# Part of a state-space scan's states summed in columns by VectorE and accumulating DMAs instead of transposed by TensorE

## What is computed

```python
u = silu(conv(in_proj_w @ ctx) + conv_b)          # [e, l]
Bm, Cm = rows of x_proj_w @ u                     # 16 x l each
delta = softplus(dt_proj_w @ dt_lo + dt_proj_b)   # [e, l]
for l:                                            # for each state n
    state[e, n] = state[e, n] * exp(delta[e, l] * A[e, n]) + delta[e, l] * u[e, l] * Bm[n, l]
    y[e, l] = sum_n state[e, n] * Cm[n, l]
y = (y + D[e] * u) * silu(layernorm(x).T)         # then transposed to [l, e]
x = x + tanh(g_xattn) * y.T
x = x + tanh(g_ffn) * (shared(ln(x)) + sum over routed e of weight_e * expert_e(ln(x)))
expert(x) = (silu(x @ W1) * (x @ Wg)) @ W2
```

## Time and profile before

| | us |
|---|---|
| median of 3 runs | 1496.21 (1495.25 to 1496.78) |
| the profiled execution | 1496.58 |
| its span, first to last instruction | 1494.5 |
| TensorE busy | 1397.6 (94%) |
| VectorE busy | 1053.1 (70%) |
| ScalarE busy | 510.0 (34%) |
| GpSimd busy | 453.6 (30%) |
| mean granted TensorE clock | 0.968 of full |

### The profile page before, as it was taken

One profiled execution on the slowest core, in us unless ns is written; L12 is line 12 of the kernel. 1 busy time (PEld: TensorE's weight loads), 2 busy tenths in 40 slices (PEclk: granted clock), 3 DMA queues, 4 the chain that ended last, 5 costly groups with the idle time before them and its releaser, 6 DMA issues.

```text
span 1494.5 us, 18163 instructions
## 1 busy us (share of the span) xinstructions
PE 1397.6 (94%) x6311; PEld 1078.6 (72%) x6311; DVE 1053.1 (70%) x1259; ACT 510.0 (34%) x855; POOL 453.6 (30%) x240
## 2 busy tenths in 40 slices
PE   8599869999999989999999979999999999999999
PEld 4244456877777776787787867787778878888887
DVE  5898855899998974588999874689999853222222
ACT  3676625544444323432322223432332211111111
POOL 3200004687777721123323211122332211111111
PEclk9599989999999999999999999999999999999999
DMA  6111634567765574455555564455555554655552
GB/s 206 43 64 57 252 121 171 204 248 272 243 244 206 212 249 141 143 192 179 177 173 181 174 247 128 143 184 179 185 176 172 184 191 156 210 194 191 189 168 84
DMA packets 90796, 266.36 MB, mean 178 GB/s; under 512 B 11472, under 2 KB 11600, under 8 KB 90336
## 3 DMA queue, kind: packets, MB, share of 16 engines
q1 hardware_dynamic: 85472, 258.39, 51.0%
q10 hardware_dynamic: 5248, 6.96, 1.3%
HBM read 207.39 MB, written 57.93 MB: 178 GB/s over the span
## 4 chain that ended last, share of the span: by engine, by line
PE 68%; DVE 18%; issue 6%; ACT 5%; DMA 2%; SPq 1%; POOL 0%; ACTq 0%; DVEq 0%; POOLq 0%
PE ps_hg L461 19%; PE ps_h L461 18%; PE ps_y L461 12%; PE ps_y L612 7%; DVE st L1098 7%; PE ps_mid L538 5%; DVE y_rows L1104 3%; ACT dA L791 2%; PE ps_h L530 2%; DVE st L1089 1%; DVE u L1000 1%; PE ps_mid L508 1%; DVE h_tmp L1224 1%; PE ps_mid L501 1%; DVE h_tmp L1219 1%
## 5 line engine op out<-in xcount | busy, mean ns | idle before, releaser
L1363 POOL TENSOR_TENSOR h_lo<-h_tmp,h_hi 128x512 fp32r<-128x512 f32 x128 | 280.8, 2194 | 781.7 <-ACT h_hi L863 781.7
L461 PE MATMUL ps_h<-x_hi,w_split 128*128 128x512 f32 x1024 | 350.8, 404 | 9.0 <-issue 4.6
L461 PE MATMUL ps_hg<-x_hi,wg_split 128*128 128x512 f32 x1024 | 349.8, 403 | 3.4 <-DVE h_tmp L1224 3.4
L1098 DVE TENSOR_TENSOR_SCAN st<-dA,st 128x1024 f32<-128x1024 f32 x128 | 298.5, 2341 | 0.0
L461 PE MATMUL ps_y<-w_split,h_hi 128*128 128x512 f32 x1024 | 258.2, 400 | 0.8 <-ACT h_hi L863 0.8
L461 PEld LDWEIGHTS ps_h<-x_hi,w_split 128*128 128x128 f32 x1024 | 195.1, 191 | 50.8 <-issue 6.9
L863 ACT ACTIVATE h_hi<-h_tmp 128x512 fp32r<-128x512 f32 x128 | 81.0, 632 | 430.6 <-DVE h_tmp L1224 430.6
L461 PEld LDWEIGHTS ps_hg<-x_hi,wg_split 128*128 128x128 f32 x1024 | 195.3, 191 | 44.4 <-issue 4.2
L461 PEld LDWEIGHTS ps_y<-w_split,h_hi 128*128 128x128 f32 x1024 | 190.3, 190 | 40.0 <-ACT h_hi L863 2.0
L1219 DVE SCALAR_TENSOR_TENSOR h_tmp<-h_tmp,ps_h 128x512 f32<-128x512 f32 x128 | 87.8, 686 | 182.8 <-ACT h_tmp L857 182.4
L461 PE MATMUL ps_hg<-x_lo,wg_split 128*128 128x512 f32 x512 | 202.1, 395 | 0.0
(11 more groups left out here) (140 smaller groups left out, 1133.5 us busy)
## 6 DMA issues: line engine op xcount, KB each, us to landing
w_split<-split_scratch SPq DMA_DIRECT2D x192, 512.0 KB, 4.9
wg_split<-split_scratch SPq DMA_DIRECT2D x96, 512.0 KB, 4.2
split_scratch<-w_split SPq DMA_DIRECT2D x64, 512.0 KB, 4.3
b_all<-xd_scratch SPq DMA_DIRECT2D x64, 256.0 KB, 4.0
split_scratch<-wg_split SPq DMA_DIRECT2D x32, 512.0 KB, 3.1
w_raw<-in_W_dram SPq DMA_DIRECT2D x14, 1024.0 KB, 7.6
wg_raw<-in_Wg_dram SPq DMA_DIRECT2D x7, 1024.0 KB, 10.0
dA<-in_x_dram SPq DMA_DIRECT2D x4, 1024.0 KB, 11.0
```

The costliest lines, as they stand in the source:

```text
L461: mm = pe.matmul(out_, lhs[a], rhs[c], start=first and q == 0, stop=last and q == len(sides) - 1)
L1098: dve.tensor_tensor_scan(flat[1], flat[0], flat[1], 0.0, ALU.mult, ALU.add).then_inc(scan_done, 1)
L1363: pool.tensor_tensor(h_lo[:, j, :], h_tmp[j % 2][:], h_hi[:, j, :].bitcast(F32), ALU.subtract).then_inc(hl_ready, 1)
```

## The change

It concerns the three batches m = 1 to 3, whose states run beside experts. Of their 16 states the even ones from 0 to 12 (seven) are no longer transposed one by one. VectorE multiplies the scanned state, in place in `st`, by C's row, broadcast by a DMA as B's is (`load_c`, `cmul`); GpSimd issues two DMAs per such state that add the two halves to `yacc` in SBUF (`sum_state`). The product with B for state n + 2, which overwrites the same half of `st`, waits for the DMA. `yacc` starts as D / 2 times u, made by ScalarE; the four blocks of matmuls against diag(D / 2) are gone for these batches. In step e = 6 the sum in `yacc` is transposed once, its four blocks between those of state 14 (`y_to_rows`), and VectorE adds it to y_rows (`sum_columns`). State 1 now starts y_rows. `yacc` takes the place of in_w and ctxT, and one of the two C buffers that of diag_D. GpSimd's loop over b is written out instead of looped. Batch 0's own states are as before.

```diff
-        in_w = sb("in_w", [P, KM, DI])
+        yacc = sb("yacc", [P, T, L])
+        in_w = yacc[:, 0:KM]
...
+        c_all = [diag_D[:].rearrange("p t l -> p (t l)"), sb("c_all1", [P, L])[:]]
...
-        ctxT = sb("ctxT", [P, KM, L])
+        ctxT = yacc[:, KM:2 * KM]
...
-        FRONT = ["xproj", "init0", "dt0", "init1", "dt1", "ccols", "dt2", "init2", "dt3", "init3", "z0", "z1", "z2", "z3"]
-        FIRST_FRONT = [name for name in FRONT if not name.startswith("init")]
+        FRONT = ["xproj", "dt0", "dt1", "ccols", "dt2", "dt3", "z0", "z1", "z2", "z3"]
+        FIRST_FRONT = ["xproj", "dt0", "dt1", "ccols", "dt2", "dt3", "z0", "z1", "z2", "z3"]
+        COLS = range(0, DS - 3, 2)
+        NCOL = len(COLS)
+        ROWS = [(n, i) for n in range(DS - 2) if n not in COLS for i in range(T)]
+        for i in range(T):
+            ROWS += [(DS - 2, i), ("y", i)]
+        ROWS += [(DS - 1, i) for i in range(T)]
         MID_FIRST = len(FIRST_FRONT) + T * DS + T
-        MID_TURN = len(FRONT) + T * DS + T + 2
+        MID_TURN = len(FRONT) + len(ROWS) + T + 2
...
-            return len(front_names(m)) + T * n + i
+            return len(front_names(m)) + (ROWS.index((n, i)) if some(m) else T * n + i)
...
+        def sums_done(m, n):
+            return 16 * (NCOL * (m - 1) + n // 2 + 1)
...
+            def load_c(m, n):
+                if n < 4:
+                    sp.wait_ge(xd_st, 16 * (m + 1))
+                else:
+                    sp.wait_ge(cmul_done, 2 * (NCOL * (m - 1) + n // 2 - 1))
+                src = xd_dram[bass.ds(m, 1)][:, bass.ds(DS + n, 1), :].rearrange("a r l -> (a r) l").broadcast_to([P, L])
+                sp.dma_start(c_all[n // 2 % 2], src).then_inc(c_ld[n // 2 % 2], 16)
+            def load_bc(m, n):
+                load_b(m, n)
+                if n in COLS:
+                    load_c(m, n)
...
-            load_b(1, 0)
-            load_b(1, 1)
+            load_bc(1, 0)
+            load_bc(1, 1)
...
-                    elif kind == "init":
-                        for et in range(T):
-                            mm = pe.matmul(ps[:, et * P:(et + 1) * P], u[:, et, i * P:(i + 1) * P], diag_D[:, et, :],
-                                           start=True, stop=True)
...
+            def y_to_rows(m, i):
+                bank, before = mid(m, sum_place(m, "y", i))
+                for h in range(2):
+                    pe.wait_ge(ysum_st[h], sums_done(m, COLS[-1]))
+                mid_free(bank, before)
+                for et in range(T):
+                    mm = pe.transpose(ps_mid[bank][:, et * P:(et + 1) * P], yacc[:, et, i * P:(i + 1) * P], ident[:])
...
-                        front(m, *{5: ("xproj", "init0"), 6: ("dt0", "init1"), 7: ("dt1", "ccols"), 8: ("dt2", "init2"),
-                                   9: ("dt3", "init3"), 10: ("z0", "z1")}.get(g, ()))
+                        front(m, *{5: ("xproj",), 6: ("dt0",), 7: ("dt1", "ccols"), 8: ("dt2",), 9: ("dt3",),
+                                   10: ("z0", "z1")}.get(g, ()))
...
-                    if 0 <= n < DS:
+                    if n < DS and n not in COLS:
                         state_to_rows(m, n, g % T)
+                    if n == DS - 2:
+                        y_to_rows(m, g % T)
...
-            def front_init(m, i):
-                if i == 0 and some(m):
-                    act.wait_ge(x1_ready, T * m)
-                bank, before = mid(m, front_place(m, f"init{i}"))
-                act.wait_ge(mid_done[bank], before + 1)
-                act.activation(y_rows[:, i, :], ps_mid[bank][:], ACT.Copy).then_inc(mid_read[bank], 1)
+            def front_init(m, et):
+                if et == 0:
+                    act.wait_ge(u_ready, T * (m + 1))
+                    if m > 1:
+                        act.wait_ge(*taken(m - 1, sum_place(m - 1, "y", T - 1)))
+                    else:
+                        act.wait_ge(inproj_done, T * NB)
+                act.activation(yacc[:, et, :], u[:, et, :], ACT.Copy, scale=half_D[:, et:et + 1]).then_inc(yinit_done, 1)
...
-                    dve.wait_ge(*taken(m, front_place(m, "init3")))
+                    dve.wait_ge(yinit_done, T * m)
...
+                if some(m) and n - 2 in COLS:
+                    dve.wait_ge(ysum_st[h], sums_done(m, n - 2))
...
+            def cmul(m, n, h):
+                odd, two, ring = n % 2, slice(2 * h, 2 * h + 2), n // 2 % 2
+                dve.wait_ge(c_ld[ring], 16 * ((NCOL + 1 - ring) // 2 * (m - 1) + n // 4 + 1))
+                dve.wait_ge(scan_done, 2 * (DS * m + n) + h + 1)
+                dve.tensor_tensor(st[odd][:, two], st[odd][:, two],
+                                  c_all[ring].rearrange("p (a l) -> p a l", a=1).broadcast_to([P, 2, L]),
+                                  ALU.mult).then_inc(cmul_done, 1)
+            def sum_columns(m, i):
+                bank, before = mid(m, sum_place(m, "y", i))
+                dve.wait_ge(*taken(m, sum_place(m, DS - 2, i)))
+                dve.wait_ge(mid_done[bank], before + 1)
+                dve.tensor_tensor(y_rows[:, i, :], ps_mid[bank][:], y_rows[:, i, :], ALU.add).then_inc(mid_read[bank], 1)
...
+                if n == 1:
+                    dve.tensor_scalar(y_rows[:, i, :], ps_mid[bank][:], c_cols[:, i, n:n + 1], None,
+                                      ALU.mult).then_inc(mid_read[bank], 1)
+                    return
...
-                if r == 0:
-                    if n >= 2:
-                        sum_rows(m, n - 2, T - 1)
-                elif 1 <= n <= DS:
-                    sum_rows(m, n - 1, r - 1)
+                before, i = (n - 2, T - 1) if r == 0 else (n - 1, r - 1)
+                if before >= 0 and before not in COLS:
+                    sum_rows(m, before, i)
+                if before == DS - 2:
+                    sum_columns(m, i)
+                if n - 1 in COLS and r < 2:
+                    cmul(m, n - 1, r)
...
+            def sum_state(m, n):
+                for h in range(2):
+                    pool.wait_ge(cmul_done, 2 * (NCOL * (m - 1) + n // 2) + h + 1)
+                    if n == 0:
+                        pool.wait_ge(yinit_done, T * m)
+                    else:
+                        pool.wait_ge(ysum_st[h], sums_done(m, n - 2))
+                    two = slice(2 * h, 2 * h + 2)
+                    pool.dma_start(yacc[:, two], st[n % 2][:, two], accum_op=ALU.add).then_inc(ysum_st[h], 16)
...
-                split = isinstance(b, int) and b == 0
+                split = b == 0
                 step_(STEPS * b, split, lambda j: power(zvar, zrstd, m) if j == 1 else None)
-                if split:
-                    for e in range(1, NE):
-                        step_(STEPS * b + e, split)
-                else:
-                    with pool.Fori(1, NE) as e:
-                        step_(STEPS * b + e)
+                step_(STEPS * b + 1, split)
+                for e in range(2, NE):
+                    first = 3 * (e - 2)
+                    def between(j):
+                        n = first + {0: 0, 2: 1, 3: 2}.get(j, DS)
+                        if n in COLS:
+                            sum_state(m, n)
+                    step_(STEPS * b + e, split, between)
...
-            with pool.Fori(1, NB - 1) as b:
+            for b in range(1, NB - 1):
```

31 lines of the change are left out of this document (18 added, 13 removed).

## The result

The changed kernel takes 1553.55 us (median of 4 runs, 1551.29 to 1555.37) against 1496.49 us beside it: ratio 1.038, 95% interval 1.0364 to 1.0396, **57 us slower**. The forecast was 1492.2 us with a range up to 1518. The profiled execution took 1551.97 us, span 1550.1.

What follows compares the result with a forecast made beforehand. TensorE (38.6 us) and VectorE (37.6 us) were taken to bound a step nearly equally, VectorE alone beside batch 0. Batches 1 and 2 gave -7.8 us, batch 0 +3.7: -4.1 us, forecast 1492.2 us, range 1466 to 1518.

Steps and rivals of the forecast that it cites:

- The D term: Shared step: four blocks of matmuls against diag_D leave TensorE, taking 3.7 us per batch off the path, all three batches.
- type A step: Steps e = 2 and 4, two column states of three: -1.2 us each beside batches 1 and 2, bounds -3.2 to +0.8.
- type B: Steps e = 3 and 5, one column state of three: -0.7 us each beside batches 1 and 2, bounds -1.9 to +0.5.
- Its waits for TensorE, 2.4 us, go: Steps e = 2 and 4: with 8 blocks fewer TensorE stops being the bound, so VectorE's 2.4 us of waits vanish.
- hidden under TensorE there: Step e = 7: VectorE's fourth addition of the transposed sum falls there and costs nothing.
- +3.6: Step e = 6: additions, collision and two transposed blocks per slot lengthen it by 3.6 us, bounds +1 to +5.
- +3.7 predicted: Steps beside batch 0, VectorE the bound: half the C products collide with weight splits; +3.7 us with the D saving included.
- Issue: ... I take 1.0 us: GpSimd's queue: issuing an accumulating DMA takes 1.0 us, between 0.33 and 1.29 us; used for its landing time.
- Rival 1: B product of state n + 2 waits for a late DMA landing, five times per batch: 1516 or 1546 us; chance 0.25.
- Rival 2: Collisions of VectorE and GpSimd at their upper bound in steps with column states: 1506 us, half the excess 1500; chance 0.15.
- Rival 3: No collisions of VectorE and GpSimd around the C product and scan: 24 us faster, 1472 us; chance 0.17.
- rival 4: TensorE is the only bound and VectorE bends, so removed blocks pay in full: 47 us faster, 1449 us; chance 0.05.

Runs made afterwards that it cites:

- the D term alone: Kernel before, no column states; ScalarE scales u by D and TensorE transposes that, instead of matmuls against a diagonal matrix: 1490.19 us, ratio 0.9957.
- The filled places: Kernel after with unread work where column states had freed TensorE: blocks of four transposes, 1539.77 us, or two matmuls for each block, 1543.09 us.
- The two runs on the DMAs: Kernel after without its 42 accumulating DMAs, 1535.57 us; kernel after with each of them cut from 512 KB to 32 KB, 1550.06 us.
- both repairs: Kernel after with the y sum's transposed blocks moved from e = 6 to e = 7 and unread transposes at TensorE's freed places: 1534.92 us, ratio 1.024.

## Why the prediction was wrong

Two slips in the sums come first, neither of weight: 1496.21 - 4.1 is 1492.1 us and not 1492.2, and TensorE waited 0.9 us in such a step by the earlier trace rows (40.02 - 39.11), not 1.4.

**The D term: right in size.** -3.7 us predicted for each batch; -2.77 - 0.82 = -3.6 us in batch 1 and -3.5 us in batch 2. Batch 0 gave 2.0 us, half. Only 2.8 us of it show in the shared step itself, where my sign asked for 3.5 to 3.7; the other 0.8 fall into e = 1. In the run with the D term alone four transposed blocks stay, and the shared step is as short, because it keeps its clock. The kernel after loses 1.6 us to the clock there as the kernel before does: its shared steps take 49.9 us in batches 1 and 2, and 48.28 us where the same step keeps its clock (run without the y blocks).

**VectorE's work: right in size too.** Work and collisions together were to make +1.2 us in a type A step, +0.8 in type B, +2.6 in e = 6. From 36.26 and 36.47 us it went to 37.06 (e = 4), 37.00 and 39.01 us: +0.8, +0.7, +2.5. The first scan behind a C product in each of these steps takes 3.38 us, as taken from the earlier trace rows; the second one of a type A step takes 2.28 us.

**The step that failed first: "Its waits for TensorE, 2.4 us, go"** (and 1.5 us in type B). They did not go: VectorE idles 5.8 us in e = 4 (42.85 - 37.06) and 4.9 us in e = 3, against 3.76 us. With 8 blocks less TensorE comes early to the one wait for a scan, idles 3.08 us and then, in e = 4 of batch 1, works at 1.2 GHz, and VectorE waits for that. In e = 3 the like stands ahead of the down part: 2.91 us of wait for h_hi, then a granted clock of 0.63 in the four microseconds from 751. I had the row for it in hand, the 2.15 us idle and 0.63 behind it, and priced it at 1.6 us for batch 0 only, "in the range". It belonged in the sum of the steps with freed places beside all three batches, even though not each of them pays (e = 2 of batch 1 and e = 4 of batch 2 kept their clock). The filled places show it: 5.0 and 2.7 us over e = 2 to 5 of batches 1 and 2, 1.3 us in e = 6 of batch 1. The clock is only a part of the miss. What a type A step takes at full clock without fillers is shown by e = 4 of batch 2: 40.11 us, where 38.8 were forecast and 40.04 stood before. VectorE idles 3.16 us in it (40.11 - 36.95): 0.81 and 1.33 us for ScalarE's tanh, 1.01 us for the gate product, which comes late because TensorE itself waited 3.08 us for the scan. Of the 2.4 us of waits 0.6 went. So of the 4.0 us by which e = 4 of batch 1 missed its forecast 2.7 are the clock and 1.3 are waits that did not go: the two engines wait for each other in turn, and neither one's work is the step.

**The y sum: "hidden under TensorE there" failed, "+3.6" held where the clock did.** Step e = 6 rose by 4.0 us in batch 2, at a clock of 1.00, and by 5.3 us in batch 1, of which 1.3 are the clock. Step e = 7, which was to stay, rose by 5.2 us in batch 1 and 3.8 us in batch 2, and 4.8 and 3.7 us of that go with the y blocks. The walk through two blocks per slot was right as a mechanism and stopped one step early: the last pair keeps both banks full into e = 7, whose first block waits 2.07 us, and the clock takes 1.6 us more.

**Batch 0: +3.7 predicted, +33.5 measured.** The step was "Issue: ... I take 1.0 us": it measured 0.88 us, but I used it only to ask whether the DMA comes in time and never added 14 of them to the queue of GpSimd, the engine whose operations block VectorE's there and are blocked by them. The two runs on the DMAs give it 16 us. The C products give 15 us: VectorE is the bound, and I had let half of them collide at 1.0 us and set the saved sums against the rest, while they themselves take 1.2 to 1.8 us there and what they lengthen are scans (VectorE busy 46.48 us in e = 4 against 40.23). The y sum gives 6 us. These add to 38, less 2.0 for D, against 33.5: they overlap. The Trainium skill (SBUF — State Buffer, section SBUF: two separate sides) calls the ports that VectorE and GpSimd share an exclusive lock, under which the loser blocks for the other's whole instruction; the scan of 6.00 us among three waiting GpSimd operations agrees. What the slow clock costs in batch 0 stays open: it was 0.90 over e = 2 to 6, and no run brought it back above 0.94 with the rest unchanged.

**Rival 1** did not happen as written: one wait of 1.96 us. The landing is 7.6 us, not 5.5, and the late landing comes out once the steps are short (28.4 us in 12 waits). The estimate by the Trainium skill (DMA: Bandwidth & Descriptors, Anatomy of one DMA) was 3.2 us for one such DMA; the trace has 7.6 for 512 KB and 5.0 for 32 KB. **Rival 2**, collisions, had the right sign and place, but priced 10 of 57 us. **Rival 3** fell with the scans of 3.38 us behind a C product, **rival 4** with VectorE, busy 37.06 of 42.85 us. Of my signs those on single operations came beside batches 1 and 2 (C products of mostly 1.2 us, the scan of 3.4 us, next to no idle time for a landing), those on whole steps did not, TensorE idles 4.4 to 5.1 us in type A where 3 to 4 were expected, and the last one, "steps lengthen beyond 40", did come.

What stays open: how batch 0's parts share their overlap, and the turn of TensorE's loop. Columns beside batches 1 and 2 only was not tried; by the steps of both repairs those batches would be 5 and 3 us over the kernel before, so nothing is to be won there.

## What to carry to other kernels

Where two engines are within a few per cent of each other, work taken from one turns into idle time of it, since each waits for the other in turn, and idle time of TensorE can come back as a slow clock: price the idle time, not only the work. When a step has a second length at a lower clock, look for an execution of the same step at full clock before giving the whole loss to the clock. An added DMA issue is an instruction on its engine's queue; add it there before asking when the DMA lands. When a change has several parts, run the part that should pay by itself: the D term alone was worth 6.4 us here, while the whole cost 57.

## What the runs showed of the hardware

- TensorE's clock fell to 0.59 with no idle time in the profile, behind small matmuls (16 rows by 512 and 48 by 16), and to 0.57 at the same place of the kernel after; in the runs with the D term alone and without the y blocks it stayed at 1.00 there. What decides it is not shown.
- A wait of 3.08 us of TensorE at the same place of two like steps was followed by a granted clock of 0.50 in one (the step 42.85 us) and 1.00 in the other (40.11 us).
- Adding 84 unread blocks to a kernel made it faster, by 14 us with transposes and by 10 us with matmuls; with either the granted clock was 1.00 over 160 us where it had been 0.95.
- An issue on GpSimd takes 0.88 us for 512 KB and for 32 KB alike; landing takes 7.6 and 5.0 us.
- A scan that takes 2.28 us elsewhere took 6.00 us among three waiting GpSimd operations.
